# Two score banks in one VectorE row maximum, in the attention of a macaron block on one Trainium2 core

## The reference, cut to what matters

```python
x = x + 0.5 * ffn(layernorm(x))             # first FFN block
x = x + linear_attention(layernorm(x))
x = x + 0.5 * ffn(layernorm(x))             # second FFN block, same weights

def ffn(hs):                                 # B=8, S=512, D=256, H=16 heads, KPH=8
    Q, K, V = heads(hs @ q_w + q_b), heads(hs @ k_w + k_b), heads(hs @ v_w + v_b)
    scores = einsum('bhsk,bhtk->bhst', Q[..., :KPH], K) / sqrt(KPH)
    attn = softmax(scores, axis=-1)          # over t, 512 columns
    mla_out = concat(attn @ V, zeros) @ o_w + o_b
    # top-2 of 8 experts for each token, each expert 256 -> 512 -> 256 with GELU
    return hs + 0.3 * experts(mla_out)
```

## Time and profile before

| | us |
|---|---|
| three runs | 2160.52 (median), 2152.19, 2161.12 |
| the profiled execution | 2161.11 |
| its span, first to last instruction | 2159.4 |
| TensorE busy | 1849.6 (86%) |
| VectorE busy | 1539.8 (71%) |
| ScalarE busy | 926.3 (43%) |
| mean granted TensorE clock | 0.927 of full |

### The profile page before, as it was taken

How to read it: one execution, slowest core, us unless ns; L and a number is a source line. 1 busy time by engine, 2 the same in 40 slices (tenths; PEclk the granted TensorE clock), 3 DMA queues, 4 the chain that set the end, 5 groups by cost and what they waited for, 6 DMA issues and landing times. The chain is left out here.

```text
span 2159.4 us, 38745 instructions
## 1 busy us (share of the span) xinstructions
PE 1849.6 (86%) x12392; PEld 1025.5 (47%) x12392; DVE 1539.8 (71%) x3941; ACT 926.3 (43%) x1694; POOL 603.3 (28%) x789
## 2 busy tenths in 40 slices
PE   1799999999949995999999983699999999769991
PEld 1443333333348883566666662133333332258880
DVE  2578888888456664788888763678898889346665
ACT  0136666666712222444444421056666666612220
POOL 2212333231236663000000001222233331246660
PEclk9789999999969997999999986589999999879995
DMA  8335333331022224111110005336333321023227
GB/s 200 62 48 124 75 75 65 64 62 29 22 68 71 71 71 146 40 41 40 41 41 11 11 11 114 68 65 137 65 67 65 73 53 23 29 90 120 81 70 243
DMA packets 146419, 154.12 MB, mean 71 GB/s; under 512 B 18828, under 2 KB 134540, under 8 KB 145868
## 3 DMA queue, kind: packets, MB, share of 16 engines
q1 hardware_dynamic: 118880, 104.35, 21.6%
q0 software_dynamic: 12928, 34.49, 4.8%
q10 hardware_dynamic: 14412, 12.79, 2.8%
HBM read 86.75 MB, written 58.34 MB: 67 GB/s over the span
## 5 line engine op out<-in xcount | busy, mean ns | idle before, releaser
L602 DVE TENSOR_REDUCE f_M<-bank 128x1 f32<-128x512 f32 x1024 | 672.7, 685 | 184.3 <-PE bank L885 174.2
L510 ACT ACTIVATE f_PT<-bank 128x512 f32<-128x512 f32 x1024 | 566.0, 607 | 264.8 <-PE bank L904 260.0
L885 PE MATMUL bank<-f_KS,f_QS 96*128 96x512 bf16 x1024 | 405.8, 403 | 59.0 <-DVE f_M L602 27.1
L904 PE MATMUL bank<-f_QS,f_KS 99*128 99x512 bf16 x1024 | 383.6, 387 | 27.5 <-ACT f_PT L510 16.8
L904 PEld LDWEIGHTS bank<-f_QS,f_KS 99*128 99x128 bf16 x1024 | 100.0, 100 | 390.6 <-ACT f_PT L510 276.7
L914 PE MATMUL bank<-f_PT,f_V 128*32 128x512 f32 x2048 | 273.8, 605 | 0.0
L885 PEld LDWEIGHTS bank<-f_KS,f_QS 96*128 96x128 bf16 x1024 | 101.9, 100 | 179.6 <-DVE f_M L602 109.5
L1146 PE MATMUL bank<-f_room,f1m_gT 128*128 x568 | 137.4, 386 | 0.1
L1146 PE MATMUL bank<-f_room,f2m_gT 128*128 x568 | 136.2, 383 | 0.3
L439 POOL DMA_INDIRECT routed_rows<-f_AO,f_rows_i x128 | 123.6, 965 | 42.1 <-issue 42.1
L1084 ACT ACTIVATE f2m_gT<-f2m_hb 128x512 f32<-128x512 f32 x71 | 44.7, 630 | 161.1 <-DVE f2m_hb L1108 158.8
(11 more groups left out here) (256 smaller groups left out, 3058.2 us busy)
## 6 DMA issues: line engine op xcount, KB each, us to landing
f_QS<-q_parts SPq DMA_DIRECT2D x192, 64.0 KB
f_KS<-k_parts SPq DMA_DIRECT2D x168, 64.0 KB
xr<-f_xr SPq DMA_DIRECT2D x16, 512.0 KB, 3.2
f_room<-in_L_ffn_w SPq DMA_DIRECT2D x2, 4096.0 KB, 22.6
fc_rows<-expert_rows SPq DMA_DIRECT2D x16, 512.0 KB, 10.9
la_rows<-expert_rows POOLq DMA_DIRECT2D x14, 512.0 KB, 5.1
q_parts<-f_q SPq DMA_DIRECT2D x16, 384.0 KB, 2.5
k_parts<-f_k SPq DMA_DIRECT2D x16, 384.0 KB, 2.5
```

The lines of the kernel that those rows point to most:

```text
L510: act.activation(PT[:, i % 8, :], score_bank(e, i)[:, :], ACT.Exp).then_inc(probs_ready, 1)
L602: dve.tensor_reduce(M[:, t, h:h + 1], SCM[(a * SC + i) % 3][:, :], AX.X, ALU.max).then_inc(scm_drained, 1)
L885: pe.matmul(SCM[(a * SC + i) % 3][:, :], QS[par][0:K_MAX, h, t * P:(t + 1) * P], KS[par][0:K_MAX, h, :], start=True, stop=True).then_inc(s ...
L904: pe.matmul(score_bank(a, i)[:, :], KS[par][0:K_EXP, h, t * P:(t + 1) * P], QS[par][0:K_EXP, h, :], start=True, stop=True).then_inc(sce_fi ...
```

## The change

One `tensor_reduce` takes the maxima of the tiles in banks 5 and 6 together (a source of 128 x 2 x 512, two columns out); the tile in bank 7 is still reduced alone. A tile in bank 5 is skipped when its turn comes, unless it is the last of its batch element; a tile in bank 6 that is the first of its element is reduced alone. The pair raises `scm_drained` by two, once, when it is done. For two neighbouring tiles to be neighbouring columns, `M` is laid out by head and tile instead of tile and head, and `split_maxima` reads it through a rearranged view. The eight banks become one PSUM tensor, with the same eight views. TensorE's and ScalarE's instructions and waits are as before.

```diff
-        M = sb("M", [P, T, H])
+        M = sb("M", [P, H, T])
...
-        SCE, SIDE, PVB, SCM = bank[0:2], bank[2:4], bank[4], bank[5:8]
+        SCM_AT = 5
+        SCE, SIDE, PVB, SCM = bank[0:2], bank[2:4], bank[4], bank[SCM_AT:8]
...
             def maximum(a, i):
-                dve.wait_ge(scm_filled, a * SC + i + 1)
-                h, t = i // T, i % T
-                dve.tensor_reduce(M[:, t, h:h + 1], SCM[(a * SC + i) % 3][:, :], AX.X, ALU.max).then_inc(scm_drained, 1)
+                n = a * SC + i
+                of_heads = M[:, :, :].rearrange("p h t -> p (h t)")
+                if n % 3 == 0 and i + 1 < SC:
+                    return
+                first = i - 1 if n % 3 == 1 and i > 0 else i
+                dve.wait_ge(scm_filled, n + 1)
+                source = banks[:, SCM_AT + n % 3 - (i - first):SCM_AT + n % 3 + 1, :]
+                dve.tensor_reduce(of_heads[:, first:i + 1], source, AX.X, ALU.max).then_inc(scm_drained, i + 1 - first)
...
-                mh = M[:, :, half * HH:(half + 1) * HH]
+                mh = M[:, half * HH:(half + 1) * HH, :].rearrange("p h t -> p t h")
...
-        bank = [ctx.enter_context(nc.psum_tensor(f"bank{i}", [P, 512], F32))[:, :] for i in range(8)]
+        banks = ctx.enter_context(nc.psum_tensor("banks", [P, 8, 512], F32))
+        bank = [banks[:, i, :] for i in range(8)]
```

More of the change, by code:

```diff
@@ L107, in region_rows, with attend_and_route @@
     return tokens + P
-def attend_and_route(nc, new_sem, tag, nth, x_in, xr_out, xs, bank, ident, tri, w, scratch, routing, dims,
+def attend_and_route(nc, new_sem, tag, nth, x_in, xr_out, xs, bank, banks, ident, tri, w, scratch, routing, dims,
                      fold, load_w2):
@@ L1858, in attend @@
                 def attend(fold):
-                    attend_and_route(nc, sem, tag, nth, x_in, xr, xs, bank, ident, tri, w, scratch, routing, dims, fold, load_w2)
+                    attend_and_route(nc, sem, tag, nth, x_in, xr, xs, bank, banks, ident, tri, w, scratch, routing, dims, fold, load_w2)
                 if nth == 0:
```

## The result

The changed kernel takes 2253.71 us (median of 4 runs, 2246.99 to 2256.76) against 2160.82 (4 runs of the kernel before): a ratio of 1.0439, 95% interval 1.0418 to 1.0460, or +93 us. The forecast was 2232, with a range of 2190 to 2262: the direction and the range hold, and the time lies 22 us above the point forecast.

A forecast was written before the change was run, and what follows sets the result against it. TensorE's queue carries the path, with VectorE's rate on it in about five groups of 16; the pair's longer loop adds 61 + 6 + 5 = +72 us, giving 2232 us, range 2190 to 2262.

The forecast's parts named there:

- The loop: From bank 6's first-score matmul through the pair to bank 5's next matmul: 0.49 + 1.22 + 0.05, so 1.76 us.
- the hand calculation: Turn followed tile by tile; three quiet groups take 10.59 us, not 9.30, 0.43 us a group more.
- The turn: Turn with e and s, bank 5's tile in its first slot: group ends move later, reaching 4.5 us at group 15.
- The other two slots: Turns with e and s whose bank 5 tile starts in another slot: 3.35 and 5.55 us longer.
- 14 turns with e and s: All turns having both e and s: 5 x 4.5 + 5 x 3.35 + 4 x 5.55, +61 us.
- turn with s alone, first block: First block's turn without e: some 12 groups end their first scores 0.75 us later, +6 us.
- the same, second block: Second block's turn without e, at TensorE's lower clock: 2.37 against 1.80 us for three maxima, ten triples, +5 us.
- rival (c): In turns with e and s, added waits drop TensorE to 1.2 GHz in an eighth: some 40 us more, 2270; chance 0.07.
- (a): VectorE is the bound and the pair relieves it: -23 us, 2138 if TensorE's waits didn't grow; chance 0.07.
- (b): The loop binds, but VectorE's existing backlog gives most back; only quiet groups' 0.43 us counts: 30 us, 2191; chance 0.14.
- (d): An instruction over two banks saves nothing; the pair costs two single lengths: 2278; chance 0.05.
- (e): Gain in groups 9 to 13 cancels loss elsewhere, no change; needs loops to cost 1.6 us a turn; chance 0.05.

The follow-up runs named there:

- half-column control: Single maxima over the first 256 of 512 columns, no pairs, against the kernel before: 2099.14 us, ratio 0.9744.
- the kernel without any pair: Changed kernel with 1024 single maxima but both of the pair's waits (held and released as pairs), against the kernel before: 2265.13 us, ratio 1.0500.

## Why the prediction was right

**The loop, right to 0.01 us.** B to A takes 1.77 us where the forecast had 1.76. The quiet group takes 3.75 us. In the hand calculation the group laid out like it, with B first, is the second of the three: 10.59 - 3.74 - 3.10 = 3.75 us.

**The turn, right to 0.4 us up to group 11.** How much later each group ends than in the turn of before, for the turn with A in its first slot that starts at 268.17 us, worked out from the starts of each group's first second score in both traces:

```
end of group      1    2    3    4    5    6    7    8    9   10   11   12   13   14   15
forecast (us)   0.45 0.45 1.2  1.5  1.5  1.5  2.2  2.2  2.6  3.2  3.1  3.7  4.3  3.9  4.5
measured (us)   0.54 0.54 1.3  1.7  1.7  1.7  2.3  2.3  2.9  3.6  3.5  5.1  6.2  5.8  6.4
```

The other two slots: forecast 3.35 and 5.55 us. Measured are 3.75 (two turns) and 5.8 (three turns) wherever the clock stayed up and the turn has an f. Two signs that I had asked for didn't come. I expected turns of 64.6 to 66.8 us with the full clock in them; several took 67 us and more, one 69.37, and the clock fell six times.

**The sum, too small by 21 us.** The parts of the 93.4 us between the two spans, from where the same instructions start in both traces (the first second score of an element opens its turn with e; the first first-score of a block opens its turn with s alone):

| part | forecast | measured |
|---|---|---|
| 14 turns with e and s | 61 | 37.5 + 41.2 = 78.6 |
| turn with s alone, first block | 6 | 6.6 |
| the same, second block | 5 | 5.5 |
| everything else | 0 | 2.7 |

The term that was mis-sized is the one of the 14 turns, by 18 us, for two reasons and a rest.

First the clock, which I had kept apart as rival (c). What stands around group 12 of the turn above, TensorE in order of time:

```profile
318.44 0.39 PE L910 MATMUL banks<-f_QS,f_KS 99*128 99x512 bf16 x1
320.05 0.39 PE L891 MATMUL banks<-f_KS,f_QS 96*128 96x512 bf16 x1 [1.22 <-DVE f_M L608]
...
320.38 1.94 PE L920 MATMUL banks<-f_PT,f_V 128*32 128x512 f32 x8
322.25 0.61 PE L910 MATMUL banks<-f_QS,f_KS 99*128 99x512 bf16 x1
322.64 0.63 PE L891 MATMUL banks<-f_KS,f_QS 96*128 96x512 bf16 x1
```

and the same time in stretches of 4 us (PE, PEld, DVE, ACT, POOL busy, granted clock, DMA share, GB/s):

```profile
316.00:320.00 4.00, 2.51 (x19) 0.84 (x11) 3.77 (x9) 2.27 (x4) 0.00 (x0) 1.00 0.58 64
320.00:324.00 4.00, 3.95 (x15) 0.86 (x15) 1.70 (x5) 0.85 (x2) 0.00 (x0) 0.57 0.10 11
324.00:328.00 4.00, 3.47 (x23) 1.05 (x21) 3.86 (x11) 2.44 (x5) 1.03 (x2) 1.00 0.00 0
```

TensorE had been busy 2.51 of 4 us, with two waits for the maxima, the last of 1.22 us. Then its clock went down to 1.2 GHz: the four `weigh` took 1.94 us in place of 1.06, and the scores 0.61 in place of 0.38. In 320 to 324 the granted clock of 0.57 means 2 x (1 - 0.57) x 4 = 3.4 us at the lower level. In the twelve turns named above (e and s, without the first of each block) I find 0 us at the lower level before and 6.8 + 13.7 = 20.5 us after, in six falls. A matmul takes nearly twice as long there, so that is at most some 10 us (an estimate: half of 20.5). The turns themselves say a little less. The five in which the clock fell lose 32.1 us together, 9.7 more than forecast, and about 8 more than if they had been off by the 0.3 us of the undisturbed ones.

I had judged (c) by the busy share of a whole turn, 88%, which came out as 87 to 89%. But the share isn't even over a turn. Five of the six falls are in groups 9 to 12, where the waits stand close together; before them TensorE had been busy 2.3 to 2.7 of 4 us, with single waits of up to 1.73 us. The sixth is in group 1 of a turn, after 2.81 of 4. Nor does the share decide it: earlier in this same turn, in

```profile
303.00:307.00 4.00, 2.27 (x16) 0.67 (x14) 3.55 (x7) 1.85 (x6) 2.50 (x3) 1.00 0.14 48
```

TensorE was busy less and kept the full clock. So a wait there could cost more than its length, but which one does isn't told by these rows. The 40 us of rival (c) don't follow from its own words either: an eighth of 14 turns with 56.4 us of matmuls in 60 holds about 100 us of them, and twice as long would cost about that much, not 40.

Second, the last turn with e and s of each block has no f, and with it none of the work that spread the tiles of groups 5 and 6 and hid the loop. I had counted it like the others. These two turns lose 6.4 and 5.9 us (61.12 and 60.55 against 54.7), not 3.35 and 4.5: 4.4 us. Groups 5 and 6 are not all of it. Against a turn with f and the same slot of A, the first of the two loses 2.7 us more: 0.8 in groups 5 and 6, 1.1 in the groups before and the rest after. In the second the groups 5 and 6 are 0.6. Why the other groups lose more without f isn't settled.

61 + 4.4 and 8 to 10 for the clock make 73 to 75. The 3 to 5 us left are the size of 0.3 us a turn, by which the undisturbed turns also miss the hand calculation (3.75 against 3.35, 5.82 against 5.55), whose steps are no finer than 0.05 us; the first turn of the second block misses it by 1.1. The 2.7 us outside the turns aren't explained. The change is 1.1 us ahead at the first block's first scores, 43.0 us behind where that block's turn with e alone starts, 47.3 at the second block's first scores, and in the last stretch it gains 0.6. Single runs of one kernel lie 10 us apart.

**The rivals.** (a) fell by its own sign, and the half-column control shows the 4.3 us a turn on which it rests. (b) would have needed the backlog of groups 9 to 13 to take the waits up; pairs in groups 8 to 15 alone cost 44 us. (d) fell by the pair's 1223 ns and by the kernel without any pair. (c) was a part of the truth, 8 to 10 us. (e) needed loops of 1.6 us a turn, and they cost 3.7 and more.

**A better version.** None of the kernels that take whole maxima beats the one before, and the runs say why. The pair saves 0.07 us of VectorE; in 336 pairs that is 17 us by the busy times, and VectorE's rate decides over a quarter of such savings: about 4 us (an estimate from the half-column control), less than a measurement can tell. To be worth its wait a pair would probably need a fourth bank for the first scores, and all eight are in use. That wasn't tried.

## What to carry to other kernels

A ring of buffers that are drained one by one must not be judged by the draining engine's time alone: taking two buffers in one instruction ties the release of the first to the filling of the second, and the loop is then the distance of the two fills + start + length of the long instruction + release. Write this loop down and compare it with the time in which the producer comes back to the same buffer; with three buffers there was no room for it, and the loss was four times the 23 us that the merged instruction could have saved. Where the producer's queue is in order, count what stands behind the held instruction, and look at the producer's granted clock where several such waits stand close together: in this kernel five of its six falls were there.

## What the runs showed of the hardware

A VectorE maximum from PSUM over two neighbouring banks takes what one stream of its length would, to about 1%: 1223 ns for 2 x 512 fp32 columns, against 684 for 512 and 421 for 256, with the next instruction 1.14 us after its start. 2 x 256 columns out of two banks, with a gap between, take 691 ns, within 1% of 512 in a row.

From the start of a first score's matmul to that of the maximum that waits for it took 0.49 us at the full clock, and from the end of the pair to the start of the matmul that waits for it 0.06 us (297.31, 297.80 and 299.02, 299.08 above).

TensorE's clock stayed at 2.4 GHz in the twelve turns of the kernel before, as in the stretch 540 to 550, busy 8.93 of 10 us. In the changed kernel it fell after 2.51 busy of 4 us, with waits of up to 1.22 us among them, and the granted clock of the next 4 us was 0.57 although TensorE was busy 3.95 of them. In 303 to 307 us it was busy 2.27 of 4 and kept the full clock.
